# Second normalisation of batches 1 to 3 moved from the causal prologue into rounds 0 to 3

## The reference, cut to what matters

```
h  = layernorm(x) * (1 + ca) + sa            # first normalisation
x1 = x + ga * attention_1(h)                 # 1 head of 128, no mask, softmax
h  = layernorm(x1) * (1 + cb) + sb           # second normalisation
# the feed-forward part, applied to h:
n  = rmsnorm(h) * g1                         # still the "second normalisation" here
q, k, v = n @ wq, n @ wk, n @ wv             # 16 query heads, 4 key/value heads of 64
q, k = rotary(q), rotary(k)
h2 = h + causal_attention(q, k, v) @ wo
y  = h2 + moe(rmsnorm(h2) * g2)              # 8 experts, top 2, capacity
out = x1 + gb * y
```

## Time and profile before

| | |
|---|---|
| median of runs | 1347.49 us |
| the profiled execution's own time | 1353.67 us |
| its span | 1351.8 us |
| TensorE / VectorE / ScalarE / GpSimd busy | 1125.3 / 1061.0 / 840.5 / 1000.6 us |
| mean granted TensorE clock, of full speed | 0.92 |
| first attention ends (x1 complete) | about 215.4 us |
| first causal score | 271.6 us |

### The profile page before, as it was taken

How to read it: one execution, slowest core, us unless ns; L and a number is a source line. 1 busy time by engine, 2 the same in 40 slices (tenths; PEclk the granted TensorE clock), 3 DMA queues, 4 the chain that set the end, 5 groups by cost and what they waited for, 6 DMA issues and landing times.

```text
span 1351.8 us, 36055 instructions
## 1 busy us (share of the span) xinstructions
PE 1125.3 (83%) x14984; PEld 842.2 (62%) x14984; DVE 1061.0 (78%) x2177; ACT 840.5 (62%) x1508; POOL 1000.6 (74%) x786
## 2 busy tenths in 40 slices
PE   4978884499999999999999999999999997600881
PEld 2767682256767667677676776676767776500881
DVE  6587757687888988889889888898888875592665
ACT  3646673378777777778777787787777884100230
POOL 2545877579988889889888898888888996226354
PEclk8889996699999999999999999999999998555996
DMA  6250010222212122122121122211211200022793
GB/s 214 49 138 2 2 51 35 74 71 59 60 46 69 39 62 56 52 56 53 48 75 37 52 61 55 60 45 56 75 37 25 57 6 2 0 83 79 211 298 141
DMA packets 49247, 90.85 MB, mean 67 GB/s; under 512 B 8896, under 2 KB 19136, under 8 KB 48832
## 3 DMA queue, kind: packets, MB, share of 16 engines
q1 hardware_dynamic: 46128, 81.21, 21.2%
q0 software_dynamic: 2960, 7.38, 2.1%
HBM read 43.96 MB, written 13.01 MB: 42 GB/s over the span
## 4 chain that ended last, share of the span: by engine, by line
PE 60%; DVE 20%; POOL 7%; issue 5%; ACT 3%; SPq 3%; DMA 2%; POOLq 0%; DVEq 0%; ACTq 0%
PE psT L1094 5%; PE psS L1164 5%; PE psS L1163 5%; PE psT L1082 5%; PE psS L1185 5%; PE psS L1186 5%; PE psS L1187 4%; PE psT L1112 3%; PE psO L1094 3%; PE psO L1164 3%; PE psO L1163 3%; POOL rows_in L716 2%; DVE pmax L1571 2%; DVE psT L1548 2%; DVE halfmax L1418 2%
## 5 line engine op out<-in xcount | busy, mean ns | idle before, releaser
L690 POOL TENSOR_TENSOR probs<-arena,probs 128x512 f16<-128x512 f32 x576 | 652.5, 1158 | 115.8 <-ACT probs L878 115.4
L878 ACT ACTIVATE probs<-arena 128x512 f16<-128x512 f32 x576 | 358.1, 622 | 0.0
L886 ACT ACTIVATE arena<-psS 128x512 f32<-128x512 f32 x384 | 228.1, 594 | 146.7 <-PE psS L1167 84.0
L1185 PE MATMUL psS<-vb,probs 128*128 128x65 f16 x2304 | 302.0, 193 | 4.2 <-POOL probs L690 1.9
L1186 PE MATMUL psS<-vb,probs 128*128 128x64 f16 x2304 | 303.5, 194 | 0.0
L1187 PE MATMUL psS<-vb,probs 128*128 128x65 f16 x2304 | 301.5, 192 | 0.0
L1185 PEld LDWEIGHTS psS<-vb,probs 128*128 128x128 f16 x2304 | 220.1, 97 | 71.9 <-issue 9.4
L1186 PEld LDWEIGHTS psS<-vb,probs 128*128 128x128 f16 x2304 | 215.4, 97 | 47.4
L1571 DVE TENSOR_REDUCE pmax<-psT 128x1 f32<-128x512 f32 (+1 forms) x305 | 193.7, 639 | 40.1 <-PE psT L1094 19.2
L1187 PEld LDWEIGHTS psS<-vb,probs 128*128 128x128 f16 x2304 | 217.0, 99 | 0.0
L1571 DVE TENSOR_REDUCE pmax<-psO 128x1 f32<-128x512 f32 (+1 forms) x207 | 139.3, 673 | 24.0 <-PE psO L1094 16.8
(11 more groups left out here) (269 smaller groups left out, 2890.0 us busy)
## 6 DMA issues: line engine op xcount, KB each, us to landing
arena<-arena SPq DMA_DIRECT2D x240, 128.0 KB, 2.4
arena<-w_exp_dram SPq DMA_DIRECT2D x40, 384.0 KB, 4.4
arena<-xnT_d SPq DMA_DIRECT2D x16, 512.0 KB, 3.5
wkv<-w_d SPq DMA_DIRECT2D x16, 352.0 KB, 4.0
rows_in<-arena POOLq DMA_DIRECT2D x1, 2580.0 KB, 21.0
arena<-rows_in SPq DMA_DIRECT2D x40, 64.5 KB, 3.3
arena<-x_dram SPq DMA_DIRECT2D x4, 512.0 KB, 5.1
hres<-x_dram SPq DMA_DIRECT2D x4, 512.0 KB, 5.1
```

Source lines behind the costliest of these rows:

```text
L690: pool.tensor_tensor(pl[:, r, :], pf[:, r, :], ph[:, r, :], ALU.subtract).then_inc(lo_P, 1)
L878: act.activation(ph[:, s % RING, :], pf[:, s % RING, :], ACT.Copy).then_inc(b_hi, 1)
L886: act.activation(pf[:, s % RING, :], score_banks[s % SCORES], ACT.Exp).then_inc(b_exp, 1)
L1185: pe.matmul(dst, high, vb[:, p, j, 0:OW], start=first, stop=False, skip_group_check=True)
```

## The change

Batches 1 to 3 leave the prologue. Their remaining parts get a round and a step in tables; each engine does its part after its own work of that step. The transposes become entries `in2` of the side work, half a batch at a time at steps 29 and 31 of rounds 0, 1 and 3. ScalarE writes the high half from the bank and VectorE the low half (in place of ScalarE's full copy and GpSimd's subtraction). The scalings of one 128x128 piece each stand at steps 8 to 15. Buffers for these parts are others (`xhl_late` on the memory of O16, a new `n2s_late`, `sqh`, and batch 3 centred within `hres`). The clear of the ones row waits for the last x1 and no longer for `with_rows(3)`. The stores stand at the end of SP's list of their round.

```
+INPUT_OF = {0: 1, 1: 2, 3: 3}
+INPUT_AT = {29: 0, 31: 1}
+NORM_V = {0: {1: ("d", 1), 12: ("b", 2), 18: ("c", 2), 33: ("d", 2)}, 1: {20: ("a", 3), 23: ("a_centre", 3), 32: ("b", 3)},
+          2: {6: ("c", 3), 28: ("d", 3)}}
+NORM_A = {0: {30: ("squares", 2, 1)}, 1: {28: ("squares", 3, 0)}, 2: {24: ("squares", 3, 1)}}
+NORM_P = {0: {3: ("power", 1, 1), 15: ("power", 2, 0), 21: ("scaled", 2), 27: ("shifted", 2)},
+          1: {2: ("power", 2, 1), 8: ("gated", 3), 14: ("with_rows", 3)},
+          2: {2: ("power", 3, 0), 12: ("scaled", 3), 18: ("shifted", 3), 32: ("power", 3, 1)}}
+OUT_FROM, SB = 8, 3
...
 # side_work(it)
+        if it in INPUT_OF and s in INPUT_AT:
+            now.append(("in2", INPUT_OF[it], INPUT_AT[s]))
...
 # SyncE
+                sp.wait_ge(xn_out, 16 * (it // HKV) + 16)
                 sp.dma_start(xs[:, p, :, :], xnT_d[it // HKV]).then_inc(loads_in[p], 16)
...
-            store_input2(1)
             spread_k(0, 0)
             spread_q(0, 0, 0)
             spread_q(0, 0, 1)
-            store_input2(2)
             spread_row(start(0, "A"), 0, 0)
-            store_input2(3)
-            sp.wait_ge(xn_out, 16 * B)
...
 # round_loads, at its end
+                if it in INPUT_OF:
+                    store_input2(INPUT_OF[it], it)
...
 # GpSimd
-            norm2_power(1, 1)
-            norm2_power(2, 0)
-            gated(3)
-            with_rows(3)
-            pool.wait_ge(xsum, B)
+            pool.wait_ge(a_x1, 2 * B)
             pool.memset(kB[HD:HD + 1, :, :], 1.0).then_inc(ones_set, 1)
             pool.wait_ge(ones_set, 4)
-            scaled(2)
-            shifted(2)
-            input2_low(1)
-            norm2_power(3, 0)
-            low_half(0, 0, 0)
-            norm2_power(2, 1)
-            low_half(1, 0, 0)
-            scaled(3)
-            shifted(3)
-            low_half(2, 0, 0)
-            input2_low(2)
-            norm2_power(3, 1)
-            input2_low(3)
+            for c in range(3):
+                low_half(c, 0, 0)
...
 # pool_round, after the step's low half
+                    if s in NORM_P.get(it, {}):
+                        norm2(*NORM_P[it][s])
...
 # ScalarE
+            def norm2_late(c, j):
+                act.wait_ge(n2_pow[1], c + 1)
+                act.activation(n2s_late[:, j, :], hres[:, c, j, :], ACT.Copy, scale=rstd2[1][:, j:j + 1]).then_inc(n2_out, 1)
...
+            def input2_high(e, bank, full):
+                c, h = e[1:]
+                act.wait_ge(side_full, full)
+                if c > 1:
+                    act.wait_ge(xn_out, 16 * c)
+                act.activation(xhl_late[:, 0, :].rearrange("d (p j) -> d j p", j=NT)[:, 4 * h:4 * h + 4, :],
+                               side_banks[bank].rearrange("d (j p) -> d j p", p=P), ACT.Copy, scale=g1T[:, 0:1]
+                               ).then_inc(xn_hi, 1)
...
 # act_round, in step s, behind the exponential and the high half of the step before
+                        if e[0] == "in2":
+                            input2_high(e, i % SB, start(it) + count(work[:i + 1]))
+                    if s in NORM_A.get(it, {}):
+                        norm2_squares(*NORM_A[it][s][1:])
+                    if it in INPUT_OF and OUT_FROM <= s < OUT_FROM + NT:
+                        norm2_late(INPUT_OF[it], s - OUT_FROM)
...
 # TensorE, prologue
-                if PROLOGUE[i] == ("q", 0, 0):
-                    pe.wait_ge(a_E, NL)
-                    turn_input2(1, psS[:, 0, :])
                 if PROLOGUE[i] == ("max", G, 0):
-                    turn_input2(2, psS[:, 1, :])
                     pe.wait_ge(ones_set, 4)
-                if PROLOGUE[i] == ("max", G + 1, 0):
-                    pe.wait_ge(n2_T, 2)
-                    turn_input2(3, psS[:, 0, :])
...
 # TensorE, fill
+                if kind == "in2":
+                    pe.wait_ge(n2_out, 1 + NT * e[1])
+                    for j in range(4):
+                        mm = pe.transpose(dst[:, j * P:(j + 1) * P], n2s_late[:, 4 * e[2] + j, :], ident)
+                    return mm
...
 # VectorE, after the first attention and in the prologue
-            norm2_d(1)
-            norm2_b(2)
-            norm2_c(2)
-                if e == ("k", 1):
-                    norm2_a(3)
-                if e == ("r", 0, 0):
-                    norm2_b(3)
-                if e == ("r", 0, 1):
-                    norm2_c(3)
-                if e == ("v",):
-                    norm2_d(2)
-                if e == ("r", 1, 1):
-                    norm2_d(3)
...
 # VectorE, read
+                elif kind == "in2":
+                    c, h = e[1:]
+                    v.wait_ge(xn_hi, 2 * (c - 1) + h + 2)
+                    high, low = (xhl_late[:, a, :].rearrange("d (p j) -> d j p", j=NT)[:, 4 * h:4 * h + 4, :] for a in range(2))
+                    ins = v.scalar_tensor_tensor(low, src.rearrange("d (j p) -> d j p", p=P), g1T[:, 0:1], high,
+                                                 ALU.mult, ALU.subtract)
...
 # vec_round
+                if it == 1:
+                    v.wait_ge(n2_s, 5)
...
+                    if s in NORM_V.get(it, {}):
+                        norm2(*NORM_V[it][s])
```

More of the change, by code:

```diff
@@ L68 @@
 ROW_AT = 5
-READER = {"max": "V", "row": "A", "k": "V", "v": "V", "q": "V", "r": "V", "turn": "V", "out": "V", "gap": "-"}
+READER = {"max": "V", "row": "A", "k": "V", "v": "V", "q": "V", "r": "V", "turn": "V", "out": "V", "in2": "V", "gap": "-"}
 def reader(entry):
@@ L82, with side_work @@
 LOW_AT = {5: 0, 15: 1, 25: 2}
-def side_work(first, last):
+INPUT_OF = {0: 1, 1: 2, 3: 3}
[7 more added lines that the diff above has]
+OUT_FROM, SB = 8, 3
+def side_work(it):
     steps = []
+    first, last = it == 0, it == NKV - 1
     for s in range(SPR):
@@ L123, in start @@
 def start(it, eng=None):
-    if isinstance(it, int) and it == 0:
-        return count(PROLOGUE, eng)
-    if isinstance(it, int) and it == NKV:
-        return start(NKV - 1, eng) + count(flat(side_work(False, True)), eng)
-    return it * count(flat(side_work(False, False)), eng) + (
-        count(PROLOGUE, eng) + count(flat(side_work(True, False)), eng) - count(flat(side_work(False, False)), eng))
-assert all(len(w) % SB == 0 for w in (PROLOGUE, flat(side_work(True, False)), flat(side_work(False, False)),
-                                      flat(side_work(False, True))))
+    return count(PROLOGUE, eng) + sum(count(flat(side_work(r)), eng) for r in range(it))
+assert all(len(w) % SB == 0 for w in [PROLOGUE] + [flat(side_work(r)) for r in range(NKV)])
 NL = B * NT
@@ L475, in _, with store_input2 @@
                 sp.dma_start(hres[:, b, :, :], x[b].rearrange("(p j) e -> p j e", p=P)).then_inc(xrow_in, 16)
-            def store_input2(c):
-                sp.wait_ge(xn_lo, c + 1)
-                sp.dma_start(xnT_d[c], xhl).then_inc(xn_out, 16)
-            store_input2(0)
-            sp.wait_ge(xn_out, 16)
+            def store_input2(c, it):
+                if c == 0:
+                    sp.wait_ge(xn_lo, 1)
+                    sp.dma_start(xnT_d[0], xhl).then_inc(xn_out, 16)
+                    return
+                own = [e for e in flat(side_work(it)) if reader(e) == "V"].index(("in2", c, 1))
+                sp.wait_ge(side_V, start(it, "V") + own + 1)
+                sp.dma_start(xnT_d[c], xhl_late).then_inc(xn_out, 16)
+            store_input2(0, None)
             for it in range(2):
                 load_round(it, it)
-            store_input2(1)
             spread_k(0, 0)
@@ L498, in round_loads @@
                     load_round(it + 2, p)
-                work = [e for e in flat(side_work(first, last)) if reader(e) == "A"]
+                work = [e for e in flat(side_work(it)) if reader(e) == "A"]
                 def row_of(h):
@@ L840, in _, with vec_read_of @@
                     input2(b - 3, psTf)
-            VEC_AT = {e: i for i, e in enumerate(x for x in flat(side_work(False, False)) if reader(x) == "V")}
-            VEC_FIRST = {e: i for i, e in enumerate(x for x in flat(side_work(True, False)) if reader(x) == "V")}
-            VEC_PRO = {e: i for i, e in enumerate(x for x in PROLOGUE if reader(x) == "V")}
+            def vec_read_of(it, e):
+                work = PROLOGUE if it < 0 else flat(side_work(it))
+                own = [x for x in work if reader(x) == "V"].index(e)
+                return own if it < 0 else start(it, "V") + own
             def high_half(c, n, p, read_at):
@@ L880, in act_round @@
             def act_round(it, p, first, last):
-                steps = side_work(first, last)
+                steps = side_work(it)
                 work = flat(steps)
@@ L892, in act_round @@
                         c = HIGH_AT[s]
-                        high_half(c, it + 1, 1 - p, start(it, "V") + (VEC_FIRST if first else VEC_AT)[ROTATED[c]])
+                        high_half(c, it + 1, 1 - p, vec_read_of(it, ROTATED[c]))
                     for e in steps[s]:
@@ L1251, in _ @@
```

(26 more changed lines are left out.)

80 lines of the change are left out of this document (42 added, 38 removed).

## The result

| | before | after |
|---|---|---|
| median of 4 runs, us | 1348.41 (1346.92 to 1352.49) | 1371.43 (1369.84 to 1373.38) |
| ratio, 95% interval | | 1.0158 [1.0137, 1.018] |
| profiled execution, us (span) | 1353.67 (1351.8) | 1369.84 (1368.0) |

The forecast of 1338.7 us and its range (1326 to 1352) are both missed. I compare the two traces in three pieces, by ScalarE's exponentials. The first one stands at 242.12 us and not at 272.33: 30.2 us earlier. From the first to the last it takes 909.5 us and not 858.5: 51.1 us longer. What follows the last is 4.7 us shorter. The sum is +16.2 us, the difference of the spans.

The account below looks back on a forecast made before the run. It took the prologue as a chain of latencies and later rounds as bound by TensorE. A gain of 28.8 us less 20 us of losses gave -8.8, so 1338.7 us from the median, range 1326 to 1352.

Parts of the forecast that it names:

- The prologue: Before round 0: first score at 242.8 instead of 271.6, a gain of 28.8 us (24 to 31).
- What the rounds pay: Rounds 0 to 3: losses of 9.5, 6, 3 and 1.5 us from the moved work, 20 us in total.
- bounds 7 and 36: Losses of the rounds: 7 from GpSimd's and TensorE's capacity; 34 to 36 with VectorE's insertions in full and some of GpSimd's.
- sign for round 0: Round 0, between key low halves: near 59 us instead of 50.95, TensorE idle on GpSimd between steps 21 and 33.
- The two transposed halves: Round 1: 8 float32 transposes, 1.06 us, and VectorE waiting for ScalarE's copies; 2.5 us with norm2_b(3).
- The rescale: Prologue, at 218.53: 3.37 us beside GpSimd's product, read as waiting for it and then running 1.1 us.
- GpSimd in round 0: From step 15: power, scale, shift and 1.1 us of lock, 7.3 us, against little slack; 6.7 us lost.
- Rival 2: Rounds: VectorE's insertions paid in full, 31 us plus 5 of GpSimd's, so 36 lost, +7, 1354.7 us; chance 0.19.
- its sign of being wrong: Rounds 0 to 3 over 30 us longer in all, with TensorE waiting mostly on VectorE's banks.
- Rival 2's mechanism: Three side banks, 0.17 us between a read's end and the next fill, let no delay be caught up.
- Rivals 1 and 3: 1: rounds' stalls overlap, losses near 9 us, 1327.7, chance 0.18; 3: prologue gains only 20, net 0, 1347, chance 0.18.

Follow-up runs that it names:

- e4_prologue: The changed kernel without the rest of the second normalisation of batches 1 to 3, so the short prologue alone; 1318.65 us, ratio 0.9747.
- e1_pairs: The changed kernel with both copies of each transposed half walking another order, four float16 neighbours written together; 1352.24 us, ratio 1.0007.
- e9_small_on_act: e1_pairs with the six small 128x8 scalars of the moved parts on ScalarE instead of VectorE; 1348.53 us, ratio 1.0.
- e10_spread: e9_small_on_act with the moved parts spread over rounds 0 to 9 instead of 0 to 3, at other steps; 1328.08 us, ratio 0.9836.
- e13_gated: Like e10_spread but small scalars on VectorE, and GpSimd's gated product of batch 3 at step 10 of round 1, not 32; 1325.21 us, ratio 0.9801.
- e3_small: The changed kernel with its six small one-input 128x8 VectorE instructions given a second SBUF input, a constant tile; 1370.9 us, ratio 1.0139.
- e12_backlog: The kernel before with one to five extra GpSimd products at step 15 of some rounds and small VectorE probes; 1375.27 us, one run.
- e5_no_in2: The changed kernel without the transposed input pieces of batches 1 to 3, the normalisation itself staying in its steps; 1347.72 us, ratio 0.9976.

## Why the prediction was wrong

**The prologue, right.** 28.8 us forecast, 28.9 read; the first key was read at 215.79, 2.05 us behind x1 (forecast 2.1), and the row maxima ended at 237.79. The two ends stand 1.7 us earlier than in the traces of before because x1 does, so it is the distances that match: 24.05 us from x1 to the row maxima, 23.8 forecast. The whole of it reaches the time when the rounds get nothing (e4_prologue).

**What the rounds pay, wrong: 20 us forecast (bounds 7 and 36), 51 measured.** By round the forecast was 9.5, 6, 3 and 1.5 us; the table gives 15.5, 19.0, 8.1 and 9.0. Two steps failed. (The prediction's own sign for round 0, near 59 us, doesn't fit its sum either, 50.95 + 9.5 = 60.45.)

*"The two transposed halves put 8 float32 transposes on TensorE ... and VectorE waits for ScalarE's copy at each: 2.5 in all with norm2_b(3)"*, and 1.5 for round 3. The term counted TensorE's transposes, gave the two copies no length of their own, and paid no regard to the address order. A half holds its bank for 5 us, and the six together cost 21.2 us (after against e1_pairs). With the other order round 3 loses 1.0 us and the forecast of 1.5 would have stood. The Trainium skill (SBUF — State Buffer, Door 1: The DMA port swizzle, the note on cachelines) says that SBUF has lines of 16 bytes and that an access crossing to a new line pays; it gives no price. The runs agree that such a write pays: 2.50 us against 0.62 for single float16 elements 16 bytes apart. By itself the rule names the place in the diff and not the size, since the float32 elements of L787, also one to a line, took 1.05 per 512.

*"The rescale ... it waited, then ran 1.1 us"*: from 218.53 I took that VectorE waits for the one GpSimd instruction under way, 1 to 2 us each. In rounds 1 and 2 an instruction waited for a whole run, 7.20 and 5.89 us, and such a wait is paid about in full: both lie in the chain that ended last, and taking one away gave 5.8 us back in round 2 (e9_small_on_act). I priced the small scalars in the rounds near nothing, and these two took 12.7 us more than 0.17 each. The rule that I weighed there (the Trainium skill, GPSIMD Engine Reference, Specifications) names who contends and says nothing of how long. The traces agree with it on who (a reduction beside a busy GpSimd took its 1.21 us, a 128x8 multiply with two SBUF inputs 0.69 instead of 0.15), and show the length.

**What is left was right in size.** 51.1 less 21.2 less 12.7 is 17.2 us, if both waits were paid in full; the forecast has some 16 beside the halves (20 less 2.5 and 1.5). Within it, GpSimd in round 0 was about as forecast: ScalarE stands 3.08 us for its shift at step 30, and with the halves mended the round loses 11.7 us (9.5 forecast). In the changed kernel the chain that ended last stays on GpSimd from 271.31 us until this shift ends at 297.3, and holds the power, the scale and the shift with 6.2 us. Timeline of ScalarE in the changed kernel, and the last piece of that chain:

```profile
297.29 1.06 ACT L771 ACTIVATE arena<-hres 128x1024 f32<-128x1024 f32 x1 [3.08 <-POOL hres L625]
```

```profile
294.94 2.33 POOL hres L625
```

e10_spread and e13_gated show that this part depends on where the work stands: in other steps and over ten rounds the whole loss shrinks to 4.6 us (863.1 - 858.5), give or take the 2 us by which round 0 varies.

**The rivals.** Rival 2 gave the sign, and its sign of being wrong came true (rounds 0 to 3 are 51.6 us longer, TensorE waiting mostly for VectorE's banks), at 36 us of losses instead of 51; its sum was built of many insertions of 1 to 2 us, while two thirds of the loss sit in six halves and two tiny instructions. It had 0.19. My upper bound of 36 was no bound, since it took each insertion at the duration of the nearest row. Rival 2's mechanism, banks filled again 0.17 us behind their read, was not tested by itself. Rivals 1 and 3 are refuted by the round lengths and by e4_prologue.

**Open.** When a VectorE instruction gets in between two of GpSimd's and when it does not. In the rounds of the changed kernel and of nine experiments (all but e4_prologue), 42 instructions of VectorE (128x8 ones, and 128x1024 ones with two SBUF inputs) met GpSimd busy with more behind: 31 took 0.34 to 2.40 us, and 11 took 5.73 to 7.59, with nothing in between. It is not the form (e3_small), the size (128x8 and 128x1024 both starve), the line (the rescale got in at 276.20 of the changed kernel, after 2.17 us) or the depth of the backlog alone (e12_backlog). The place repeats: the same two instructions starve in e1_pairs, e3_small, e5_no_in2 and after. How it ends is seen in all eleven: VectorE gets in where GpSimd's run ends. In the changed kernel GpSimd then had no input for 6.79 us, which fits that the stall itself had held it back. That round 0's remaining loss in e1_pairs is GpSimd's time is read from the chain and was not separated by a run of its own.

## What to carry to other kernels

Cost a copy by its address order and its type, not by its count alone, and look in the trace for one that writes the same way: for each write ask whether neighbours in the walk are neighbours in memory, and let the read take the step. An instruction that VectorE must slip in between GpSimd's needs a place where GpSimd is seen idle in the trace; where it has a run, the bound is the length of the run and not of one instruction. And moving work out of a latency-bound prologue into full rounds paid here when it went a piece or two a round: the same steps cost 51 us in four rounds and, with the other walk and other places, 4.6 in ten.
